# Two selection planes summed by TensorE in place of an XOR tree on VectorE, and a sort phase on even and odd planes

## The reference

```python
vals = jnp.where(nd[..., None], x[:, None, :, :], jnp.inf)
s = jnp.sort(vals, axis=2)
for tau, w in zip((0.25, 0.5, 0.75), (0.25, 0.5, 0.25)):
    pos = tau * max(nv - 1, 0);  lo, hi = floor(pos), ceil(pos)
    agg += w * (v_lo + frac * (v_hi - v_lo))       # s at lo and at hi
h = relu((x + agg) @ W1 + b1);  y = (h @ W2 + b2) * mask
```

## Time and profile before

| | us |
|---|---|
| median of three runs | 3918.02 |
| the profiled execution | 3918.85 |
| its span | 3916.7 |
| up to the first tile of graph 0 | 562.5 |
| graph 0 to the next | 140.4 |
| a steady graph (8) | 187.8 |
| of it the select stretch, 4 tiles | 22.3, 23.7, 27.2, 25.9 |

### The profile page before, as it was taken

The page is one execution under the profiler, slowest core; times in us unless marked ns, Lnnn a source line. Parts: engine busy times, 40 slices in busy tenths (PEclk is TensorE's granted clock), DMA queues, the critical chain, the costliest instruction groups (busy, mean ns, idle before and its releaser), DMA issues. The chain is left out here.

```text
span 3916.7 us, 43928 instructions
## 1 busy us (share of the span) xinstructions
PE 2599.7 (66%) x14799; PEld 1087.3 (28%) x14922; DVE 3533.4 (90%) x6052; ACT 1762.6 (45%) x2295; POOL 56.6 (1%) x47
## 2 busy tenths in 40 slices
PE   0000032868686878777777878687868686877897
PEld 0000011323232232323232323232323232223665
DVE  7999989999999999999999999999999999965676
ACT  2112342636464645455554546463636364543232
POOL 0005000000000000000000000000000000000000
PEclk6555565889797988888888889898979797988777
DMA  1000000223132323232323222232323132322111
GB/s 24 0 23 20 0 6 18 39 45 67 27 65 36 61 31 61 32 59 34 58 36 56 37 53 41 48 46 44 51 40 66 26 67 33 50 51 36 42 34 32
DMA packets 242541, 156.06 MB, mean 40 GB/s; under 512 B 126472, under 2 KB 227994, under 8 KB 242330
## 3 DMA queue, kind: packets, MB, share of 16 engines
q1 hardware_dynamic: 238202, 152.36, 22.6%
q10 hardware_dynamic: 4128, 1.05, 0.2%
HBM read 39.07 MB, written 13.63 MB: 13 GB/s over the span
## 5 line engine op out<-in xcount | busy, mean ns | idle before, releaser
L902 ACT ACTIVATE hot<-bcast,eq_bias 128x1024 bf16<-128x1024 f32 x744 | 826.5, 1111 | 576.3 <-PE bcast L560 574.2
L572 PE MATMUL rows<-hot,table 128*64 128x512 bf16 x4608 | 704.7, 414 | 31.6 <-DVE prod L1218 28.5
L1218 DVE SCALAR_TENSOR_TENSOR prod<-near,iota_b,rows 128x512 f32<-128x512 bf16 x768 | 568.8, 744 | 154.9 <-PE rows L572 94.2
L548 PE MATMUL ring<-member,neigh_t 128*128 128x512 bf16 x1955 | 541.4, 413 | 172.2 <-ACT words L876 63.6
L559 PE MATMUL bcast<-idx_t,sel_a 128*128 128x512 f16 x744 | 308.8, 415 | 193.9 <-ACT hot L902 182.6
L581 PE MATMUL found_bank<-prod,sum_to 128*64 128x512 f32 x1536 | 432.4, 632 | 4.4 <-DVE prod L1218 4.4
L1278 DVE TENSOR_TENSOR picked<-picked 128x6144 uint16<-128x6144 uint16 (+2 forms) x192 | 387.4, 2018 | 0.7
L572 PEld LDWEIGHTS rows<-hot,table 128*64 128x64 bf16 x4608 | 220.5, 113 | 481.5 <-issue 408.4
L475 PE MATMUL ring<-ident,swapped 128*128 128x128 f32 x32 | 6.4, 367 | 504.0 <-DVEq L1074 504.0
L548 PEld LDWEIGHTS ring<-member,neigh_t 128*128 128x128 bf16 x2048 | 180.7, 104 | 564.7 <-issue 212.7
L560 PE MATMUL bcast<-idx_t,sel_a 128*128 128x512 f16 x744 | 306.9, 412 | 0.0
(11 more groups left out here) (325 smaller groups left out, 4253.1 us busy)
## 6 DMA issues: line engine op xcount, KB each, us to landing
near<-idx_bt SPq DMA_DIRECT2D x768, 128.0 KB
late<-in_adj_dram SPq DMA_DIRECT2D x16, 1024.0 KB, 5.6
adjt_d<-late SPq DMA_DIRECT2D x16, 512.0 KB, 2.7
adj_l<-adjt_d SPq DMA_DIRECT2D x16, 512.0 KB, 5.9
adj_s<-adjt_d SPq DMA_DIRECT2D x16, 512.0 KB, 3.5
parts_d<-parts SPq DMA_DIRECT2D x6, 512.0 KB, 5.1
table<-parts_d SPq DMA_DIRECT2D x192, 16.0 KB, 2.2
out_dram<-x_all SPq DMA_DIRECT2D x4, 512.0 KB, 3.8
```

The lines of the kernel that those rows point to most:

```text
L548: ins = mm(ring[u % 2][:, :], kept_t[:, j, P * i:P * i + P], member[:, j, n // 2, 512 * (n % 2):512 * (n % 2) + 512], start=(j == 0), stop ...
L572: ins = mm(rows[u % 2][C * h:C * h + C, :], table[:, s, 2 * g8 + h, :], hot[:, u % HOT, h, :], start=(s == 0), stop=(s == 2))
L902: run(hot[:, u % HOT].rearrange(flat), spread_bank(l, u)[0][:, 0:2, :].rearrange(flat), ACT.Relu, bias=eq_bias[:, :]).then_inc(S["hot_read ...
L1218: stt(out=prod[:, u % DEEP, :], in0=near[:, u % NEAR, :], scalar=iota_b[:, :], in1=rows[u % 2][:, :], op0=ALU.is_equal, op1=ALU.mult).then ...
```

## The change

*Selection.* Planes 0 and 3 leave the XOR tree. Plane 0 is now the difference of running counts (`sizes`, f16); TensorE sums `picked[:, 3]` over 15 groups with an identity as weights, and 1024 times `below` plus `picked[:, 0]` over 15 groups with two identities. ScalarE copies the two sums, 128 x 192 each, out of `dense_bank` into `result`.

*Sort phase.* Constants are made early in the space of `parts`, by GpSimd and VectorE, written to DRAM and read back after the sort. The p = 1 steps of the replay run on `perm_2`, where even and odd elements are separate planes. The preparation of graph 0 stands inside the replay. Ranks are turned in f16.

```diff
+SUM_AT = (4, 5, 6, 4)
+size_sum, first_sum = dense_bank[:, 0:TAUS * C], dense_bank[:, TAUS * C:2 * TAUS * C]
 # SyncE
+            sp.wait_ge(S["stage_ready"], 1)
+            sp.dma_start(consts_d, stage[:, 0:CONSTS]).then_inc(S["stage_out"], 16)
...
             load_adj(0)
+            sp.dma_start(consts[:, :], consts_d).then_inc(S["consts_in"], 16)
 # GpSimd: fills before the sort; the affine_select chain after parts_out is gone
+            made(g.iota(column, [[1, C], [0, 32]], ...))
+            made(g.iota(shift, [[0, C], [1, 32]], base=-16, ...))
...
 # TensorE
+            def sum_first(b, i):
+                pe.wait_ge(S["first_picked"], NT * b + i + 1)
+                wait(pe, S["sums_ev"], 2 * (NT * b + i))
+                plane = picked[:, 3].bitcast(BF16)
+                for g in range(G - 1):
+                    ins = mm(first_sum.rearrange("p (k c) -> p k c", k=TAUS), identb[:, :], plane[:, :, C * g:C * g + C], start=(g == 0), stop=(g == G - 2), ...)
+                ins.then_inc(S["sums_ps"], 1)
+            def sum_size(b, i):
+                pe.wait_ge(S["size_picked"], NT * b + i + 1)
+                for g in range(G - 1):
+                    mm(total_of, ident_k, below[:, i % 2, :, C * g:C * g + C], ...)
+                for g in range(G - 1):
+                    ins = mm(total_of, identh[:, :], plane[:, :, C * g:C * g + C], ...)
+                ins.then_inc(S["sums_ps"], 1)
             def select(b, l):
...
                 for n in range(2, CW):
                     chunk(b, 1, n)
                     units(l, min(n - 1, LEAD[1]))
+                    if n == 4:
+                        sum_first(b, 0)
+                        sum_size(b, 0)
                 for i in range(1, NT):
                     for s in range(10):
                         if i + 1 < NT and s < CW:
                             chunk(b, i + 1, s)
                         units(l, min(LEAD[i] + AHEAD[i] + s, LEAD[i + 1]))
+                        if s == SUM_AT[i] - 1:
+                            sum_first(b, i)
+                        if s == SUM_AT[i]:
+                            sum_size(b, i)
 # ScalarE
+            def keep_sums(b, i):
+                act.wait_ge(S["sums_ps"], 2 * (NT * b + i) + 2)
+                run(result[:, 3, i, :, :]..., first_sum, ACT.Copy).then_inc(S["sums_ev"], 1)
+                run(result[:, 0, i, :, :]..., size_sum, ACT.Copy).then_inc(S["sums_ev"], 1)
...
                 units(l, 6)
+                keep_sums(b, 0)
                 mask(b, 1, 0)
...
                         units(l, min(level + s, LEAD[i + 1] + 2))
+                        if s == SUM_AT[i] + 1:
+                            keep_sums(b, i)
 # VectorE, select
                 dve.wait_ge(S["cw_ev"], NT * CW * b + CW * i + 2)
+                wait(dve, S["sums_ps"], 2 * (NT * b + i))
-                did(v.tensor_copy(words[:, 0, 0:C], group_tag[:, 0, :]))
-                did(tt(words[:, 0, C:], cnt[:, 0:last], group_tag[:, 1:, :].rearrange(flat), ALU.add))
+                did(v.tensor_copy(sizes[:, 0:C], cnt[:, 0:C]))
+                did(tt(sizes[:, C:], cnt[:, C:last], cnt[:, 0:last - C], ALU.subtract))
...
-                did(tt(change[:, :, 0:last], words[:, :, 0:last], words[:, :, C:], ALU.bitwise_xor))
+                did(tt(change[:, 1:3, 0:last], words[:, 1:3, 0:last], words[:, 1:3, C:], ALU.bitwise_xor))
...
                 place(2)
+                tt(starts[:, :, 0:last], starts..., first_at..., ALU.mult).then_inc(S["first_picked"], 1)
+                place(3)
                 if i:
                     dve.wait_ge(S["mask_made"], MASKS * b + i)
-                pick(2)
-                place(3)
-                did(tt(starts, starts, first_at..., ALU.mult))
-                place(4)
                 if i == 0 and b:
                     dve.wait_ge(S["idxT_ps"], TURNS * b)
+                tt(picked[:, 0]..., below..., sizes..., ALU.mult).then_inc(S["size_picked"], 1)
+                place(4)
                 pick(1)
                 place(5)
-                tt(picked[:, 0], below[:, i % 2], change[:, 0, :]..., ALU.mult).then_inc(S["mask_used"], 1)
+                tt(picked[:, 2], below[:, i % 2], change[:, 2, :]..., ALU.mult).then_inc(S["mask_used"], 1)
                 place(6)
-                a = picked[:, :, :, :].rearrange("p w k n -> p (w k) n")
+                a = picked[:, 1:3].rearrange("p w k n -> p (w k) n")
 # VectorE, replay
+                    if e == twos:
+                        tell("twos_done")
+                        did(v.tensor_copy(perm[:, 0:PAIRS // 2, :].rearrange("q a (k t) -> q a t k", t=2), perm_2[:, 0:PAIRS // 2]))
+                        dve.wait_ge(S["perm_made"], PAIRS + 1)
+                    if p == 1:
+                        plo = perm_2[:, :, r, 0:m].unsqueeze(3)
+                        phi = (perm_2[:, :, 0, (d + 1) // 2:(d + 1) // 2 + m] if r else perm_2[:, :, 1, 0:m]).unsqueeze(3)
...
+                    if e == 21: ... clear_own(0)
+                    if e == 22: middles(0)
+                    if e in (25, 27): drop(0, ...)
+                    if e in (29, 30): keep(0, ...)
+                    if e == 33: limits(0)
-            then(v.tensor_copy(ranks, perm[:, :, :]))
 # VectorE, before bits_start
+                    dve.wait_ge(S["sums_ev"], 2 * (NT * t_of + NT))
```

More of the change, by code:

```diff
@@ L45, with fields @@
 TURNS = K + K // 2
+FIELDS = (("sel_a", 1024, F16), ("upper", 256, BF16), ("group_id", 512, F16), ("first_tag", 512, BF16), ("ident_k", 64, BF16),
+          ("sum_to", 512, F32), ("one_u", 32, U16), ("ones_b", 1, BF16), ("eq_bias", 1, F32), ("iota_b", 1, F32))
+CONSTS = sum(n for _, n, _ in FIELDS)
+def fields(t):
+    at, views = 0, {}
+    for name, n, dt in FIELDS:
+        views[name] = t[:, at:at + n] if dt == F32 else t[:, at:at + n].bitcast(dt)
+        at += n
+    return views
 def comparators(n):
@@ L163, in build @@
                 size += PAIRS * m * p
[L164 to L166 removed]
+            swapped = ss("swapped", [P, -(-size // 4) * 4], U8)
             swap = ss("swap", [P, 2, PAIRS * N // 2], F16)
@@ L169, in build @@
             perm = ss("perm", [P, PAIRS, N], F16)
+            perm_2 = ss("perm_2", [P, PAIRS, 2, N // 2], F16)
+            twos = sum(1 for step in steps if step[0] == 1)
             place = ss("place", [P, N], F32)
@@ L431, in _ @@
[L431 to L441, removed]
-            made(g.affine_select(out=sel_a[:, :], in_=sel_a[:, :], compare_op=ALU.is_ge, fill=0.0, base=31 - C * 32,
-                                 pattern=[[-1, C * 32]], channel_multiplier=32))
@@ L444, in _ @@
-            made(g.affine_select(out=sum16[:, :], in_=sum16[:, :], compare_op=ALU.is_ge, fill=0.0, base=15,
-                                 pattern=[[16, 8]], channel_multiplier=-1))
-            here()
-            made(g.tensor_tensor(sel_a[:, :], sel_a[:, :], sel_a2, ALU.add))
-            for g8 in range(GROUPS):
-                made(g.tensor_copy(sum_to[:, g8, 8 * g8:8 * g8 + 8], sum16[:, :]))
-            here()
             made(g.memset(table[:, :, :, :], 0.0))
@@ L724, in region @@
                 issued[0] = 0
-            pe.wait_ge(S["rankT_ev"], PAIRS)
-            region(None, 0, None, None)
+            turn_adj(0)
+            count_neighbours(0)
+            for i in range(NT):
+                count_up(0, i)
+            for j in range(NT):
+                both_ways(0, j)
+            count_kept(0)
+            turn_ranks()
+            pe.wait_ge(S["member_ready"], NT)
+            for n in range(CW):
+                chunk(0, 0, n)
             for b in range(B):
@@ L820, in _ @@
             run(mask_t[:, :, :].rearrange(flat), bcast[:, 0, 0:NT * B], ACT.Copy).then_inc(S["mask_ready"], 1)
+            act.wait_ge(S["cdone"], 1)
+            for a in range(PAIRS):
+                run(perm_2[:, a], place[:, :].rearrange("q (k t) -> q t k", t=2), ACT.Copy).then_inc(S["perm_made"], 1)
             stays = 0
@@ L996, in region @@
                 spread_to[0] = 0
-            region(None, 0, None, None)
+            replay()
+            act.wait_ge(S["consts_in"], 16)
+            for n in range(CW):
+                chunk(0, 0, n)
             for b in range(B):
@@ L1536, in region @@
                 restart()
-            region(None, 0, None, None)
+            replay()
+            for j in range(NT):
+                members(0, j)
             for b in range(B):
```

235 lines of the change are left out of this document (145 added, 90 removed).

## The result

| | before | after |
|---|---|---|
| median of the runs | 3918.9 us (3916.9 to 3919.9, 4 runs) | 4023.5 us (4021.9 to 4026.3, 4 runs) |
| span of the profiled execution | 3916.7 us | 4020.1 us |
| ratio | | 1.0268 (95%: 1.0251 to 1.0286) |

The account below looks back on a forecast made before the run. It took TensorE and ScalarE's chain to bound the select stretches with lookups, VectorE following closely. +170 there, -12 in graph 0 and -43 in the sort phase gave +115 on 3918.85 us: 4033, forecast 4030 (likeliest case 3975 to 4080).

Parts of the forecast that it names:

- TensorE's time per tile: Select stretch: 45 added matmuls of 192 columns at 0.083 us, 3.75 us a tile, 15.0 us a graph.
- The landing: Select stretches with lookups: sums delay the lookups behind them, +11.35 us a graph, +170 us over 15 graphs (66 to 221).
- VectorE's slack at the end: End of the fourth tile: VectorE was later than the lookups by 3.4 us, taken off the delay.
- VectorE's saving buys nothing there: Select stretches with lookups: VectorE's 15.2 us less work a graph gains nothing, since it waits in the value unit.
- Graph 0: Select stretch without lookups, where VectorE sets the time: -12 us (-10 to -15).
- Sort phase: Before graph 0: separate even and odd planes, their merge and graph 0's preparation moved into the replay, net -43 us (-50 to -30).
- the first replay step: Sort phase: first of nine replay steps, reading from an odd element, stays slow, near its old 8.5 us.
- The rest of the phase: Sort phase: graph 0's preparation moved from behind the replay into it, 31 us against 40.1, -9 us.
- The sums fill TensorE's waits: Rival, select stretches: sums run in TensorE's idle time, +4.4 us a graph, 3930 us in all; chance 15%.
- VectorE binds: Rival, select stretches: VectorE sets the length, TensorE takes the sums for nothing, -11 us a graph, 3698 us; chance 12%.
- The planes run at the fast rate: Sort phase's first nine replay steps: -36 us; the rival without the double rate: about -8, 4060 us, chance 5%.
- costs 0.083 us and not 0.16: Rival, select stretches: strided or lower-clock sums cost 0.16 us a matmul, +13 us more a graph, 4230 us; chance 4%.

Follow-up runs that it names:

- one-group kernel: The changed kernel with each of TensorE's sums cut from 15 groups to one, 3 matmuls of 192 columns a tile in place of 45: 3828.9 us.
- the fastest kernel: The changed kernel with both sums in graph 0 alone; in graphs 1 to 15 only the first-position sum, in the fourth tile, otherwise the old selection: 3818.7 us.

## Why the prediction was right, point by point

**TensorE's time per tile: right.** The slope between the rows of 64, 128 and 512 columns gave 0.083 us for a matmul of 192; the spacing in the trace is 0.083 ((1.41 - 0.25) / 14, from the rows of 15 above and 0.25 as the mean duration of one), and the two experiments that remove and add matmuls pay 0.078 and 0.087 for each. The busy figures foretold for the stretch, over 100 and about 80, are 101.36 and 80.65. The longest waits of VectorE in tiles 1 and 2 were put at the third and fourth last value; they are 3.20 us at the third last and 1.0 at the fourth, and the longest of all, 4.67, is at value 3.

**The landing: right, with one slip that stands in two terms.** The delays foretold for lookups 3, 4, 8 and 18 were 3.75, 4.25, 7.7 and 11.45; they are 3.65, 4.1, 7.8 and 11.5. In the fourth tile the lookups were put at +3.3 and are at +2.1 (13.6 less 11.5), and VectorE's slack at the end was put at 3.4 and is 2.3 (13.6 less 11.3 in graph 8). Both terms come from where lookup 32 was thought to stand in the kernel before. The forecast let TensorE and ScalarE keep their pace of 3.98 us for two units up to there, 22.07 us from lookup 21. The trace of the kernel before has 23.26, because VectorE was late: lookups 23 to 27 each start 0.1 us after the end of the value two units before. Values 21 and 22, lookups 23 and 24, and lookup 32:

```profile
2078.06 0.74 DVE L1218 SCALAR_TENSOR_TENSOR prod<-near,iota_b,rows 128x512 f32<-128x512 bf16 x1
...
2080.42 0.73 DVE L1218 SCALAR_TENSOR_TENSOR prod<-near,iota_b,rows 128x512 f32<-128x512 bf16 x1
```

```profile
2078.95 0.84 PE L572 MATMUL rows<-hot,table 128*64 128x512 bf16 x6 [0.37 <-DVE prod L1218]
...
2081.30 0.84 PE L572 MATMUL rows<-hot,table 128*64 128x512 bf16 x6
...
2097.78 0.84 PE L572 MATMUL rows<-hot,table 128*64 128x512 bf16 x6
```

In the changed kernel no lookup is held up so, and from lookup 21 to 32 it takes 25.30 us, for 22.07 + 3.3 in the forecast; in the one-group kernel it takes 22.25. So the +3.3 was right as what the sums add to the chain itself, and the slip cancels in the sum by construction and not by luck: 110.3 on average for 110.5. It hid, however, that VectorE set the pace in the fourth tile of the kernel before, which is what the fastest kernel uses. ScalarE's two evictions, taken at 0.5 us from a row of 128x256, are 0.33 and 0.34 with 0.21 between their starts, 0.55.

**VectorE's saving buys nothing there: right but for the end of the stretch.** It was worked out as 15.2 us a graph and is 14.1 (94.73 - 80.65). The kernel with 14 us of it put back loses 2.6, about the slack of 2.3, which the sum of the forecast does take off.

**Graph 0: right, a little low.** -13.9 for -12 (-10 to -15). I had feared that the matmuls would run at 1.2 GHz; the granted clock of this stretch rose from 0.72 to 0.91, so most ran at 2.4.

**Sort phase: -47.6 for -43; the step that failed is the first replay step.** I held that a step that starts on an odd element cannot run at the fast rate, which rested on the Trainium skill (VectorE: DVE Perf Modes, section Mode 2x_1P) and on no row. The timeline of VectorE:

```profile
292.03 1.23 DVE L1220 TENSOR_TENSOR delta<-perm 128x2040 f16<-128x2040 f16 x1
293.29 1.22 DVE L1222 TENSOR_TENSOR delta<-delta,swap 128x2040 f16<-128x2040 f16 x1
294.55 1.23 DVE L1224 TENSOR_TENSOR perm<-perm,delta 128x2040 f16<-128x2040 f16 x1
295.69 1.21 DVE L1225 TENSOR_TENSOR perm<-perm,delta 128x2040 f16<-128x2040 f16 x1
...
327.09 1.23 DVE L1220 TENSOR_TENSOR delta<-perm 128x2048 f16<-128x2048 f16 x1
...
332.01 1.32 DVE L1211 COPY perm<-perm 128x2048 f16<-128x2048 f16 x1
334.59 1.22 DVE L1220 TENSOR_TENSOR delta<-perm 128x2032 f16<-128x2032 f16 x1 [1.25 <-ACT perm L914]
```

The step takes 4.9 us like one of 2048 that starts on an even element, and the nine take 40.0 (292.03 to 332.01) for the 43 of the forecast and the 78.8 of the earlier trace rows. The Trainium skill asks for 4-byte alignment there; the measurement decides against it for this form. The merge is 2.6 us for 2.4: VectorE's half takes 1.32 us, and then it waits 1.25 for ScalarE's half, which takes 2.50. The rest of the phase, graph 0's preparation moved into the replay, is -11.1 for -9: the other 36 steps with it take 160.3 us for 151.3, and from there to the first tile are 20.0 us for 40.1. The early constants run on VectorE from 9.01 to 16.25 us, and the first sort step starts at 20.13 (20.05 in the earlier trace rows): hidden, as foretold.

**The rivals.** "The sums fill TensorE's waits" is true of less than 1 us of the 15: the changed kernel's stretch is 13.0 us above the one-group kernel's, for 168 matmuls at 0.083, 13.9. Of the fourth tile's part, 0.43 had been counted, and 42 x 0.083 less 0.43, 3.06, is what that tile pays (26.98 less 23.93, 3.05). "VectorE binds" is true only in graph 0 and in the fourth tile: it held up TensorE there in the kernel before, and it ends the stretch. The planes run at the fast rate, and a matmul of the sums costs 0.083 us and not 0.16.

## What to carry to other kernels

Before work is moved from the busiest engine to another, read the stage where it lands, not the shares of the whole span: TensorE, with 66% there, had 11 us of 99 left in that stage, and what was put into its queue ahead of the lookups delayed all of them. Find the chain's owner by making each candidate's work dearer in turn (here 15.6 us paid for 15 on TensorE, 2.6 for 14 on VectorE; ScalarE was left out), and tile by tile, since the owner changes within a stretch; the edit can still pay where the relieved engine is last and nothing of the loaded engine's queue follows.

## What was not expected of the hardware

- VectorE's two-input operation on 2040 f16 elements whose one source starts on an odd element takes 1.23 us, and 1.21 where the destination starts there too; one of 2048 on even starts takes 1.23 as well.
- A VectorE copy of 2048 f16 elements from the planes to every second element takes 1.32 us, 0.1 more than the contiguous operations of that size.
- Stretches with the same instructions and the same busy times last some 86.5 or 88.2 us, from kernel to kernel and from graph to graph. Eight matmuls some 34 us into them take 1.10 us or 1.97, by the level of TensorE's clock at that moment, and a lookup that VectorE waits for stands behind them. In the two stretches shown above TensorE had been idle for 2.61 us before the slow form and for 1.12 before the fast one. What selects the level was not tried.
